# Fourth attention: the router ranks four tiles at a time in place of eight

## The reference, cut to what matters

```
x      = x + tanh(g_xattn[3]) * attention3(layernorm(x), ctx)     # 16 heads of 8, stablemax
tokens = layernorm(x)                                             # 8192 x 128
logits = tokens @ Wg                                              # 8 experts
idx    = argmax(softmax(logits), axis=1)
mask1  = one_hot(idx, 8)
locations1 = cumsum(mask1, axis=0) - 1       # how many earlier tokens chose the same expert
mask1  = mask1 * (locations1 < 1024)         # capacity; later tokens are dropped
x      = x + tanh(g_ffn[3]) * combine(experts(dispatch(tokens, idx, locations1)))
```

## Time and profile before

| what | us |
|---|---|
| median of three runs | 2580.41 (2577.57 to 2588.39) |
| the profiled execution, its own time | 2576.2 |
| its span, first to last instruction | 2574.4 |
| DVE busy over the span | 1824.5 (71%) |
| PE busy over the span | 2163.7 (84%) |
| POOL busy over the span | 1212.3 (47%) |
| steady part of the fourth attention | some 2088 to 2392 |
| first instruction of the last expert phase | 2430.1 |

### The profile page before, as it was taken

How to read it: one execution, slowest core, us unless ns; L and a number is a source line. 1 busy time by engine, 2 the same in 40 slices (tenths; PEclk the granted TensorE clock), 3 DMA queues, 4 the chain that set the end, 5 groups by cost and what they waited for, 6 DMA issues and landing times. The chain is left out here.

```text
span 2574.4 us, 78265 instructions
## 1 busy us (share of the span) xinstructions
PE 2163.7 (84%) x32233; PEld 1658.0 (64%) x32243; DVE 1824.5 (71%) x5057; ACT 1357.1 (53%) x2507; POOL 1212.3 (47%) x1728
## 2 busy tenths in 40 slices
PE   6999999999977959995555899995799867887597
PEld 5878878788765737773444677773466546666375
DVE  4777777777773648885895689887455479999454
ACT  3555555555533338883997555551122168878232
POOL 1333433433444521113775135556466667887444
PEclk9999999999998969997777899996899968878599
DMA  7320000000007511110000011111555322332363
GB/s 201 113 105 24 27 24 26 24 20 20 20 20 200 158 56 57 58 45 4 1 1 11 29 42 52 53 46 59 150 162 161 98 84 73 94 93 71 96 184 104
DMA packets 213956, 184.51 MB, mean 72 GB/s; under 512 B 33420, under 2 KB 189654, under 8 KB 213600
## 3 DMA queue, kind: packets, MB, share of 16 engines
q1 hardware_dynamic: 194144, 142.52, 19.1%
q0 software_dynamic: 19456, 36.99, 4.2%
HBM read 102.01 MB, written 72.68 MB: 68 GB/s over the span
## 5 line engine op out<-in xcount | busy, mean ns | idle before, releaser
L609 POOL DMA_INDIRECT slots<-row,put x256 | 257.9, 1007 | 193.0 <-issue 126.7
L1893 PE MATMUL experts_H<-experts_xs_t,experts_w 128*128 128x512 f32 x576 | 266.3, 606 | 6.6 <-DMA experts_b<-in_F_b 2.6
L1067 ACT ACTIVATE l_prob_t<-l_Z 128x512 f32<-128x512 f32 x256 | 132.2, 602 | 148.6 <-PE l_Z L1181 116.6
L1419 POOL TENSOR_TENSOR l_var_eps<-l_mv,eps 128x1 f32<-128x1 f32 x64 | 12.2, 191 | 412.7 <-DVE l_mv L1500 412.7
L1911 PE MATMUL experts_Y<-experts_w,experts_hid 128*128 128x128 f32 x1664 | 197.8, 275 | 3.5 <-DVE experts_y L1841 2.6
L1758 POOL DMA_INDIRECT rows<-experts_y,experts_idx x160 | 155.5, 972 | 91.6 <-DVE experts_y L1837 51.1
L1911 PEld LDWEIGHTS experts_Y<-experts_w,experts_hid 128*128 128x128 f32 x1664 | 191.7, 192 | 5.4 <-issue 5.4
L1455 DVE TENSOR_REDUCE l_top<-l_S 128x16 f32<-128x1024 f32 x64 | 78.3, 1224 | 160.4 <-PE l_S L1598 160.4
L987 DVE TENSOR_REDUCE l_top<-l_X 128x32 f32<-128x2048 f32 x64 | 146.5, 2289 | 53.5 <-PE l_X L1188 36.4
L1893 PEld LDWEIGHTS experts_H<-experts_xs_t,experts_w 128*128 128x128 f32 x576 | 106.3, 195 | 116.1 <-issue 107.7
L898 POOL TENSOR_TENSOR l_var_eps<-l_mv,eps 128x2 f32<-128x2 f32 x96 | 24.0, 250 | 307.1 <-DVE l_mv L957 221.4
(11 more groups left out here) (326 smaller groups left out, 6023.5 us busy)
## 6 DMA issues: line engine op xcount, KB each, us to landing
experts_w<-in_F_w SPq DMA_DIRECT2D x104, 256.0 KB, 2.9
l_ctx_t<-in_ctx_t SPq DMA_DIRECT2D x96, 128.0 KB, 2.4
early_q_m<-l_q_t SPq DMA_DIRECT2D x384, 32.0 KB, 1.8
experts_xs<-slots SPq DMA_DIRECT2D x40, 264.0 KB, 3.0
slots<-l_empty SPq DMA_DIRECT2D x16, 536.0 KB, 4.0
experts_xs<-slots SPq DMA_DIRECT2D x16, 536.0 KB, 4.5
slots<-l_empty SPq DMA_DIRECT2D x16, 520.0 KB, 6.1
experts_xs<-slots SPq DMA_DIRECT2D x16, 520.0 KB, 4.4
```

The lines of the kernel that those rows point to most:

```text
L609: pool.indirect_dma_start(self.slots, bass.IndirectOffsetOnAxis(ap=g.put[c][:, tile:tile + 1], axis=0), g.row[:, tile, self.sent_cols], No ...
L1067: nc.scalar.activation(prob_t[:, t.par(PROB), r, :], Z[:, r, :], ACT.Exp).then_inc(prob_done, 1)
L1893: nc.tensor.matmul(H[:, c, :], w1_s[:, t.par(2), c, :], xs_t[:, t.par(2), :], start=True, stop=True).then_inc(h_filled[c], 1)
```

## The change

One argument of one call is changed, so that the fourth attention's batches hold four tiles:

```diff
-        attention_split(nc, g, "l3", 3, "stable", head=rows2, router=(t["F3_wg"], None, "gated", slots3), together=8, out=out)
+        attention_split(nc, g, "l3", 3, "stable", head=rows2, router=(t["F3_wg"], None, "gated", slots3), together=4, out=out)
```

## The result

The kernel with batches of four tiles takes 2595.71 us (median of 20 runs, 2583.4 to 2601.91), the one before 2585.59 in the same comparison (20 runs). The ratio is 1.0041, 95% interval [1.0027, 1.0055]: slower by 0.41%, some 10.5 us. A second comparison gave 1.0032 [1.0015, 1.0050], 6.2 us by the medians. The forecast was +4.7. The direction, the price of the chains, the gain at the end and the class "within 0.5%" were right. The forecast in absolute terms, 2585.1, was off by 10.6, and 5.2 of that is the base alone: the three runs that it started from had a median of 2580.41 where 20 have 2585.59.

A forecast was written before the change was run, and what follows sets the result against it. DVE was taken to bound the steady part, POOL's scatters the end. Chains +12.1, cover -2.3, end -5.1 made +4.7 us (rounded), added to the runs' median 2580.41: 2585.1 us, 8-in-10 range 2577 to 2596.

The forecast's parts named there:

- the class "within 0.5%": Whole kernel: a difference under 0.5% (12.9 us) cannot be told from none; chance 0.83.
- What bounds the kernel: Fourth attention: DVE limits up to about 2407 us, busy 244.56 of 267.25 us in 27 windows; POOL's scatters limit after.
- The price of a chain: Steady part: a narrow choice chain costs a step 1.32 us, a narrow slot chain 0.72; net +12.1 us.
- The end: After step 38: POOL's run of 16 scatters becomes 12, 4 x 1.287 = -5.1 us.
- These waits swallow 1.0 and 1.3 us: -2.3: Steps 15 and 35: DVE's low-clock waits for the weighted sum hide part of the new choice chains, -2.3 us.
- Rival A: Fourth attention: ten to sixteen more low-clock steps, about 0.75 us each, give +10, in all +14.7, 2595 us; chance 0.16.
- B: Steady part: waits for POOL and PE hide the new chains, leaving the end's -5.1 us, 2575.3 us; chance 0.10.
- C: End: gain lost, later `put` stalls POOL or experts' first load waits elsewhere; +9.8 and more, 2590.2 us; chance 0.09.

The follow-up runs named there:

- the filler: 20 extra matmuls, results unused, in steps 7 to 36 where the matrix engine waits for L1016; kernel before: 2572.95 us, 0.9962; four tiles: 2582.1 us, 0.9999.
- the small-batch kernel: Against the kernel before: eight tiles for the first 24 items, four for the last 8, each scatter in its right step; 2579.33 us, ratio 0.9982.
- the kernel with wide, small batches and filler: Batches of 16, 16, 8, 8 and four times 4 tiles, double scatters from the 33rd step, 20 extra matmuls; 2565.22 us, 0.9929 against the kernel before.

## Why the prediction missed the size

**What bounds the kernel: right.** DVE in the steady part, POOL's scatters at the end.

**The price of a chain: right.** 1.33 and 0.73 us measured for 1.32 and 0.72. In sum +12.1 forecast, +11.3 measured with the filler, where no window is at 0.50.

**The end: right.** -5.1 forecast, -5.6 in the profile, undone when the offset is put back.

**"These waits swallow 1.0 and 1.3 us: -2.3": wrong, and it is the step that failed.** I had taken DVE's waits of 1.01 and 1.89 us in the earlier trace rows as fixed places in which new chains could hide, and priced the case that they move at 2.3 us and no more. But low-clock steps are not fixed. They are steps 16, 23 and 36 in the one profile before and 10, 14 and 26 in the other. With four tiles there are six in each profile. A chain that meets one is partly hidden (12.83 against 12.35 for a plain low step), but the low step costs more than it hides. So there was no net cover: where the forecast had -2.3, the profiles have +6.0 and the times +1.1 (-2.5 to 4.8).

In terms of the profiles the term was 8.3 us off. The chains (0.8 less than forecast) and the end (0.5 less) give 1.3 back, which makes the 7.0 us between the forecast's +4.7 and the profiles' 17.3 - 5.6 = +11.7. In terms of the times it comes to 3.4 - 1.3 = 2.1 of the 3.6 that lie between +4.7 and 8.3, and the rest is inside the noise. So the step that failed is shown, but not how much it missed by: 3.4 us by the times, 8.3 by the profiles, and since both profiles of the kernel before are quick ones I would not rely on the larger figure.

**Rival A had the right mechanism with a wrong price and, in the profiles, a wrong count.** It had 0.75 us for each low step and ten to sixteen more of them; the profiles hold three more, at 1.8 to 2.8. The price was in reach: in the earlier trace rows the low plain step is 11.37 - 9.51 = 1.86 longer than its neighbour. The 0.75 rested on a pace of 10.63 us from L1016 to L1016 at "low clock". The first 2.03 us of that stretch had a granted clock of 0.93 and only the rest 0.50. A round wholly at the low clock, PE in the changed kernel:

```profile
2221.01 2.01 PE L1155 MATMUL l_Z<-early_q_m,l_k_t 32*64 32x256 f32 x32
...
2226.98 3.61 PE L1238 MATMUL l_X<-l_val,l_soft 128*64 128x18 f32 x64
...
2232.85 2.01 PE L1155 MATMUL l_Z<-early_q_m,l_k_t 32*64 32x256 f32 x32
```

From L1155 to L1155 it is 11.84 us, well above the 10.5 of the new mean step; I had them equal. In the first 22 windows, fewer matmuls in a microsecond went with more windows at 0.50: two and three before, four and four with four tiles, nine with two. There were none once the idle stretch was filled. The rule of the Trainium skill (TensorE: Matmul & The Clock Gate, Part 1: The HAM clock gate), that the gate follows how busy the array has been, spoke against this change, and these runs agree with it.

**Rivals B and C fell.** Up to the last five steps every chain shows in full in every high-clock step, and POOL never waited for `put` at the end: its idle marks there are issue, or the scatter before.

**What stays open.** How much of the change's cost is the low clock: +6.0 by the profiles, +1.1 by the times. The filler's gain on eight tiles is 10 to 11 us in the times and 5.2 in the windows. More low-clock steps in the typical run than in the two profiled ones would explain both, and the clocks on record and the small-batch kernel's windows speak for it; but the windows of the timed runs are not on record, and the mean clock covers the other phases too. Why the matrix engine's clock falls in just these steps is not shown either.

## What to carry to other kernels

A batch of small vector operations is nearly all fixed cost: halving the columns from 64 to 32 took 0.32 us off 2.36, so halving a batch brings the bill from 2.36 to 2 x 2.04 = 4.08. Where the end of a phase wants small batches and its middle wants large ones, give them different sizes. And where the matrix engine waits for another engine in every step, look at the granted clock of each step before hiding anything in its waits: there, a few idle-time matmuls were worth 10 us, more than this change cost. And before a difference of a few microseconds is read from two profiles, see where their executions lie among the timed ones.

## What the runs showed of the hardware that I had not expected

An indirect DMA on POOL, 0.97 to 1.1 us elsewhere, took 2.91 us when it began 0.3 us behind the start of DVE's long two-input add, which lasts 2.28. Later starts inside the add took less, and all ended alike: in the kernel with wide, small batches and filler one began 0.49 us behind the add and took 2.64, another 1.24 behind and took 1.91. Both ended 3.1 us after the add's start, some 0.9 us after its end. POOL's small L621 at the end of the changed kernel does the same: 2.91 us beside an add, 0.72 without. A choice chain in a low-clock step is partly hidden after all, 12.83 against 12.35 for a plain one at the same clock, so the chain's 1.33 shows as 0.48; it is the low step itself that costs.
